# A graph network on one core: ScalarE instead of SP begins the loads of the source one-hots, three steps ahead instead of two

## The chip, the cores and the metric

The kernel runs on one core of one Trainium2 chip. The metric is the time of the whole program on the device in microseconds (us), as the median of several runs. Apart from that there is one profiled execution, from which all rows come. In the profile PE is TensorE, PEld its weight load, DVE VectorE, ACT ScalarE, POOL GpSimd and SP the engine that only issues transfers; a q behind a name (ACTq, SPq) marks work of that engine's sequencer, such as issuing a DMA.

## What is computed

The reference applies four graph networks one after the other to 12,500 nodes with 64 features each, over the same 212,500 edges (source, destination, type 0 to 3, weight), and normalizes the node rows after each:

```python
edge_index = jnp.stack([src, dst])
x = _layernorm(x + _L0_gnn_ref(x, ..., src, dst, edge_type_4), axis=-1)   # 4 steps: typed messages, GRU cell
x = _layernorm(x + _L1_gnn_ref(x, edge_index, ...), axis=-1)              # 2 GIN layers
x = _layernorm(x + _L2_gnn_ref(x, ...), axis=-1)                          # GCN, batch norm
x = _layernorm(x + _L3_gnn_ref(x, edge_weight, ...), axis=-1)             # weighted mean of neighbours
```

What they share is the costly part, a gather by source and a sum by destination:

```python
msgs = transformed[etypes, src]
a = jax.ops.segment_sum(msgs, dst, num_segments=num_nodes)
```

## The kernel before

A setup (the first 3,690 us) sorts the edges into slots and writes one-hot matrices of their sources to HBM (src_onehots). Then come nine passes over all edges, p = 0 to 8: four steps of the first network, three for the second (the last layer takes two), one for the third, one for the fourth. A pass needs the node rows of the pass before: all of them lie in SBUF as rows_now, three bf16 parts per value.

A pass has two interleaved loops. **Steps** (102 a pass, class Step) do the gather by matrix product: a step has 8 pairs, each of two matmuls (L963) of a one-hot matrix with a slice of rows_now into one of two PSUM banks ps_pair; ScalarE copies each bank to the buffer raw (copy_pair, L1164), and after the eighth pair issues one DMA that writes raw to HBM, `bounce` (move_out, L1170). There are two raw buffers, and step n + 2 may use that of step n when its write has landed (raw_written). A step's one-hots, 256 KB, lie in one of three buffers, step n in buffer n mod 3 (oh_landed tells that they are there). **Tiles** (98 a pass, class At) do the sum by destination: tile jj reads its messages back from bounce in another order (load_msgs, L657, three buffers), GpSimd gathers left-over rows (L808), VectorE makes one-hots of destinations, TensorE sums them in ps_agg (L977 to L1006), and a chain of small operations makes the new node row: VectorE sums, TensorE turns, ScalarE copies (L1184), TensorE's first product (L1040 to L1042), ScalarE's gate (L1190), VectorE's candidate and so on to a row, whose three parts ScalarE (L1233, L1241) and VectorE (L1708) make and SP stores (L672).

Steps run 8 ahead of tiles (AHEAD_G). At a pass's start steps 0 to 7 run alone; after that tile jj runs together with step jj + 8, pair by pair, on TensorE and on ScalarE alike. The last eight tiles have no step.

Each engine runs its own list in order. SP's for a pass: wait for the last stores and for the sums of the last tile, load rows_now in seven pieces (L700, one semaphore each; in pass 8 a store of rows_now, L704, instead, after the semaphore ch_lo, which GpSimd's L834 counts up), four loads of edge records (L648), two loads of one-hots, then for each of the first eight steps one more, the load for step n + 2 when step n - 1 is summed:

```python
for a in range(AHEAD_G):
    s = Step(GSTEPS * p + a)
    if s.n > 0:
        sp.wait_ge(pair_summed, s.pairs())
    load_oh(Step(s.n + 2))
    if a == G_TILES:
        load_msgs(at, 0)
```

After that, for each tile: wait for the tile two before, load records and messages, wait for pair_summed, load one-hots, wait for the row parts of the tile three before and store them. TensorE's pair 0 of a step waits for oh_landed, and the first steps of passes 1 to 7 also for their piece of rows_now (rows_loaded). ScalarE's list for a tile (one_tile, L1243) is: copies 0 and 1, L1241, L1184, copies 2 and 3, L1190, copies 4 and 5, the candidate, copies 6 and 7, the write L1170, L1233; passes 3, 6 and 8 have a square root (L1215) in place of L1233 there.

DMAs that SP issues go to one queue, those of ScalarE to another, those of GpSimd to a third; all are worked off by the same 16 DMA engines.

Of the kernel before, what the change touches and what calls it, by code (L numbers as in the profile page):

```python
# [9 lines left out]
P = 128  # L10
# [29 lines left out]
G_TILES = 6  # L40
# [34 lines left out]
def build(nc, x, src, dst, edge_type, edge_weight, g_W, g_b, g_w_ih, g_w_hh, g_b_ih, g_b_hh,  # L75
# [472 lines left out]
    def _(sp):  # L548
# [85 lines left out]
        sp.wait_ge(full_known, 1)  # L634
        sp.sem_inc(setup_done, 1)

        def load_oh(s):
            sp.dma_start(oh_words[s.buf()], src_onehots.ap()[ds(s.group() * P, P),
                                                             s.chunk() * CHUNK * P // 2:(s.chunk() + 1) * CHUNK * P // 2]
                         ).then_inc(oh_landed[s.buf()], 16)  # L640

        def load_weights(at, more):
            n = (at.jj + more) % 3
            sp.dma_start(grec[n][0:ROWS], slots.ap()[ds(at.d(more) * TILE_SLOTS, TILE_SLOTS), :]
# [30 lines left out]
        def one_tile(at):  # L675
            sp.wait_ge(tile_summed, at.tiles(CREDIT_T - 1))
            sp.sem_inc(sp_ran, 1)
            known = isinstance(at.i, int)
            if at.p == P_SAGE and not (known and at.jj + 1 >= NT):
                load_weights(at, 1)  # L680
            if not (known and at.jj + 4 >= NT):
                load_recs(at, 4)
            if not (known and at.jj + 1 >= NT):
                load_msgs(at, 1)
            if has_step(at):
                s = step_of(at)
                sp.wait_ge(pair_summed, s.pairs())
                sp.sem_inc(sp_ran, 1)
                if not (known and at.jj + AHEAD_G + 2 >= GSTEPS):
                    load_oh(Step(s.n + 2, s.i))  # L690
            if not (known and at.jj <= 2):
                store_rows(At(at.p, at.jj - 3, at.i))

        def one_pass(p):
# [12 lines left out]
                load_recs(at, a)  # L707
            if p == P_SAGE:
                load_weights(at, 0)
            for a in range(2):  # L710
                load_oh(Step(GSTEPS * p + a))
            for a in range(AHEAD_G):
                s = Step(GSTEPS * p + a)
                if s.n > 0:
                    sp.wait_ge(pair_summed, s.pairs())
                load_oh(Step(s.n + 2))
                if a == G_TILES:
                    load_msgs(at, 0)
            one_tile(At(p, 0))
            one_tile(At(p, 1))  # L720
            one_tile(At(p, 2))
# [415 lines left out]
    def _(act):  # L1137
# [29 lines left out]
        def move_out(s):  # L1167
# [2 lines left out]
            act.dma_start(bounce.ap()[ds(s.group() * ROWS, ROWS), s.chunk() * SB * RUN:(s.chunk() + 1) * SB * RUN],  # L1170
                          raw[s.raw()][0:ROWS].rearrange("p i b f -> p (i b f)")).then_inc(raw_written[s.raw()], 16)

        def copy_turned(at):
            p = at.p
            if p == P_GIN2A:
                return
            act.wait_ge(sum_turned, turns(at))
            if p < P_GIN1:
                to, frm = turned[:, :], ps_turn[:, 0:3 * P]
            elif p in (P_GIN2B, P_SAGE):  # L1180
                to, frm = turned[0:H, 0:2 * P], ps_turn[0:H, 0:2 * P]
            else:
                to, frm = turned[0:H, 0:P], ps_turn[0:H, 0:P]
            a_(to, frm, ACT.Copy).then_inc(turned_copied, 1)  # L1184
# [58 lines left out]
        def one_tile(at):  # L1243
# [27 lines left out]
            one_pair(7)  # L1271
            if s is not None:
                move_out(s)
            if prev is not None:
                (root if normed else high)(prev)

        act.wait_ge(ones_set, 1)
        for p in range(NPASS):
# [3 lines left out]
            if p == P_SAGE:  # L1282
# [7 lines left out]
                for n in range(NCH + 2):  # L1290
# [11 lines left out]
                    if n >= 2:  # L1302
                        at = slice((n - 2) * CH, (n - 1) * CH)
                        act.wait_ge(ch_rest, n - 1)
                        a_(rows_now[:, at, H:2 * H], sq_of[:, at, :], ACT.Copy).then_inc(ch_mid, 1)
            for a in range(AHEAD_G):
                for m in range(PAIRS):
                    copy_pair(Step(GSTEPS * p + a), m)
                move_out(Step(GSTEPS * p + a))
            one_tile(At(p, 0))  # L1310
            long_loop(act, p, 1, one_tile)
            end, normed = At(p, NT - 1), p in (3, P_GIN2B, P_SAGE)
# [684 lines left out]
```

## Time and profile before

| | |
|---|---|
| median of 3 runs | 12191.25 us (12191.2 to 12294.9) |
| profiled execution | 12181.28 us, span 12179.4 us |
| mean granted TensorE clock | 0.764 of full speed |
| busy | PE 60%, PEld 43%, DVE 51%, ACT 36%, POOL 54% |
| DMA | 2042.70 MB, mean 168 GB/s; SP's queue 1117.02 MB, ScalarE's 689.26 MB |
| loads of one-hots | 918, 256.0 KB each, by SP |

The span is the time from the first to the last instruction of the profiled execution. A share is an average over the setup, in which the DMA engines do little, and nine passes of 850 to 1,050 us.

### The profile page before, as it was taken

How to read it: one execution, taken by the hardware profiler on the slowest of the kernel's cores; microseconds unless marked ns; L12 is line 12 of the kernel's file. 1: busy time of each engine (PE TensorE's matmuls, PEld its weight loads, DVE VectorE, ACT ScalarE, POOL GpSimd, SP SyncE). 2: the span in 40 equal slices, each digit the busy share in tenths (PEclk: the TensorE clock that was granted, in tenths of full speed). 3: DMA queues.
4: the chain of work that ended last, by engine and by line, in shares of the span. 5: the costliest groups of instructions: out<-in, count | busy, mean ns of one | idle time of the engine just before them, and what ended most of it. 6: DMA issues, size and time to landing. Idle time of an engine off the chain costs nothing.

```text
span 12179.4 us, 174906 instructions
## 1 busy us (share of the span) xinstructions
PE 7330.7 (60%) x53873; PEld 5276.8 (43%) x53874; DVE 6165.4 (51%) x20158; ACT 4414.1 (36%) x11121; POOL 6612.2 (54%) x6335
## 2 busy tenths in 40 slices
PE   3333333333326877777777776666666776664999
PEld 0000000000005765666666664554445554543888
DVE  6555555554545665655656772222223332224998
ACT  0000000000004555545547774554444554443444
POOL 3555555555544655555555554555664444554666
PEclk6666666666658998988998997886766776776999
DMA  2110100000018988988988887888987777885888
GB/s 92 38 32 28 31 27 23 31 28 31 28 36 227 252 229 242 241 225 240 238 230 230 227 214 220 233 236 226 253 243 202 207 207 201 224 229 152 226 226 205
DMA packets 1207353, 2042.70 MB, mean 168 GB/s; under 512 B 431620, under 2 KB 895979, under 8 KB 1200318
## 3 DMA queue, kind: packets, MB, share of 16 engines
q1 hardware_dynamic: 878942, 1117.02, 35.7%
q10 hardware_dynamic: 126656, 689.26, 16.3%
q0 software_dynamic: 200864, 225.45, 9.7%
q8 instruction: 449, 7.36, 0.3%
q14 instruction: 442, 3.62, 0.1%
HBM read 1246.93 MB, written 784.10 MB: 167 GB/s over the span
## 4 chain that ended last, share of the span: by engine, by line
PE 39%; DVE 18%; another core or an unknown queue 15%; issue 14%; ACT 8%; DMA 2%; DVEq 2%; SPq 1%; POOL 1%; ACTq 0%; POOLq 0%
PE ps_pair L963 13%; DVE work L1460 6%; ACT work L1164 6%; PE ps_agg L980 5%; DVE work L1455 3%; PE ps_agg L977 3%; PE ps_agg L983 3%; PE ps_agg L997 2%; PE ps_gate L1040 1%; DVE work L1614 1%; PE ps_gate L1042 1%; PE ps_agg L1000 1%; PE ps_agg L1006 1%; DVE work L1537 1%
## 5 line engine op out<-in xcount | busy, mean ns | idle before, releaser
L808 POOL DMA_INDIRECT work<-node_rows,work x4410 | 4722.3, 1071 | 3649.5 <-issue 1175.0
L1164 ACT ACTIVATE work<-ps_pair 120x384 bf16<-120x384 f32 x7344 | 3375.0, 488 | 5559.2 <-PE ps_pair L963 4899.5
L963 PE MATMUL ps_pair<-rows_now,work 128*128 128x192 bf16 x14688 | 2734.2, 277 | 2093.8 <-issue 888.8
L792 POOL DMA_INDIRECT slots<-work x1862 | 1832.8, 984 | 1721.1 <-DVE work L1518 1168.3
L963 PEld LDWEIGHTS ps_pair<-rows_now,work 128*128 128x128 fp8e4 x14688 | 1257.3, 105 | 2902.0 <-issue 2786.2
L1460 DVE CUSTOM_DVE_ANT_0 work<-work,ps_agg 128x384 bf16<-128x384 bf16 x1862 | 1021.4, 551 | 1487.0 <-remote 1306.3
L889 PE MATMUL ps_agg<-work,not_above 128*128 128x384 bf16 x1764 | 750.7, 426 | 1669.8 <-issue 1260.2
L889 PEld LDWEIGHTS ps_agg<-work,not_above 128*128 128x128 bf16 x1764 | 176.8, 100 | 2545.2 <-issue 1595.8
L1595 DVE TENSOR_TENSOR work<-iota_bf,dl_all 120x2048 bf16<-120x2048 bf16 x882 | 1074.5, 1218 | 14.6 <-POOL rows_now L834 7.3
L891 PE MATMUL ps_agg<-work,above 128*128 128x384 bf16 x1862 | 799.9, 435 | 468.1 <-DVE work L1455 358.7
L980 PE MATMUL ps_agg<-work 120*128 120x192 bf16 x6272 | 1021.4, 300 | 28.5 <-DMA work<-bounce 24.8
L997 PE MATMUL ps_agg<-work 128*128 128x192 bf16 (+1 forms) x7840 | 925.6, 251 | 0.0
L977 PE MATMUL ps_agg<-work 120*128 120x192 bf16 (+1 forms) x6272 | 847.3, 261 | 13.3 <-DMA work<-bounce 11.3
L980 PEld LDWEIGHTS ps_agg<-work 120*128 120x128 bf16 x6272 | 718.8, 121 | 72.1 <-issue 30.4
L997 PEld LDWEIGHTS ps_agg<-work 128*128 128x128 bf16 x7840 | 691.8, 99 | 5.3 <-issue 1.0
L1614 DVE TENSOR_SCALAR work<-iota,work 128x512 bf16<-128x512 int16 x1960 | 596.6, 371 | 47.2 <-DMA work<-slots 46.8
L1455 DVE TENSOR_SCALAR work<-iota,work 128x384 bf16<-128x384 int16 x1862 | 606.4, 330 | 3.8
L977 PEld LDWEIGHTS ps_agg<-work 120*128 120x128 bf16 x6272 | 589.6, 104 | 27.7 <-issue 15.5
L1659 DVE TENSOR_REDUCE agg_sb<-ps_agg 128x64 f32<-128x192 f32 x392 | 134.9, 344 | 865.1 <-PE ps_agg L1002 701.7
L1000 PE MATMUL ps_agg<-work 128*128 128x192 bf16 x1960 | 540.7, 290 | 3.9 <-DMA work<-node_rows,work 3.8
L1646 DVE TENSOR_REDUCE agg_sb<-ps_agg 128x256 f32<-128x768 f32 x392 | 371.6, 948 | 252.3 <-PE ps_agg L997 212.2
L983 PE MATMUL ps_agg<-work,hs 120*128 120x192 bf16 x4704 | 466.7, 249 | 4.7 <-DMA work<-bounce 3.3
(300 smaller groups left out, 8965.2 us busy)
## 6 DMA issues: line engine op xcount, KB each, us to landing
bounce<-work ACTq DMA_DIRECT2D x918, 727.5 KB
work<-bounce SPq DMA_DIRECT2D x882, 727.5 KB
work<-src_onehots SPq DMA_DIRECT2D x918, 256.0 KB
work<-node_rows,work POOLq DMA_INDIRECT x4410
work<-lo_rows SPq DMA_DIRECT2D x17, 2880.0 KB
node_rows<-stage SPq DMA_DIRECT2D x686, 48.0 KB
rows_now<-node_rows SPq DMA_DIRECT2D x42, 768.0 KB, 8.5
slots<-work POOLq DMA_INDIRECT x1862
```

The source lines that it names most:

```text
L792: pool.indirect_dma_start(out=slots.ap(), out_offset=bass.IndirectOffsetOnAxis(ap=addr[par][:, t, n:n + 1], axis=0), in_=win[par][t][:, n, ...
L808: pool.indirect_dma_start(out=ring[:, at.slot3() * LB + b, 0:3 * H], out_offset=None, in_=table_of(at.p), in_offset=bass.IndirectOffsetOnA ...
L889: mm(acc, not_above[:, :], hot[t][(n - 1) % 3], start=False, stop=True, skip_group_check=True)
L963: last = mm(bank[:, a * 3 * H:(a + 1) * 3 * H], oh[s.buf()][:, 2 * m + a, :], rows_now[:, s.chunk() * CHUNK + 2 * m + a, :], start=a == 0, ...
L977: mm(acc[:, k * AGG:k * AGG + width], doh_one[at.half()][0:ROWS, b * P:(b + 1) * P], rhs, start=b in (0, 2 * SB), stop=False)
L980: mm(acc[:, 0:3 * H], doh_one[at.half()][0:ROWS, b * P:(b + 1) * P], rhs, start=b == 0, stop=False)
L983: mm(acc[:, 0:3 * H], doh_three[at.half()][0:ROWS, (a * GB + b) * P:(a * GB + b + 1) * P], rhs, start=a + b == 0, stop=False)
L997: last = mm(acc[:, k * AGG:k * AGG + width], ohs[:, (b * K + k) * P:(b * K + k + 1) * P], rhs, start=False, stop=end and k % 2 == 1)
L1164: a_(raw[s.raw()][0:ROWS, m // 2, 2 * (m % 2):2 * (m % 2) + 2, 0:3 * H], ps_pair[m % 2][0:ROWS, 0:6 * H].rearrange("p (b f) -> p b f", b=2 ...
L1455: v.tensor_scalar(hot[t][n % 3], iota512[:, 0:NCLS], key[:, t, n:n + 1], None, ALU.is_equal).then_inc(hot_made[t], 1)
L1460: v.tensor_tensor_reduce(out=junk[(2 * n + t) % 3], in0=hot[t][n % 3], in1=ps_agg[t][:, 0:NCLS], scale=1.0, scalar=0.0, op0=ALU.mult, op1= ...
L1595: last = v.tensor_tensor(to, numbers(ROWS, GB), spread(dl_all[0:ROWS, ds(at.d(more), 1), :].rearrange("p o n -> p (o n)"), ROWS, GB), ALU. ...
```

## The change

The loads of the one-hots leave SP's list and stand in ScalarE's. At a pass's start ScalarE issues the loads of steps 0, 1 and 2, and after the write of each step n the load of step n + 3, whose buffer is that of step n. ScalarE has then copied all eight pairs of step n, so no further wait is needed. In the first eight steps SP no longer waits for anything but the writes that load_msgs needs.

```diff
@@ SP @@
-        def load_oh(s):
-            sp.dma_start(oh_words[s.buf()], src_onehots.ap()[...]
-                         ).then_inc(oh_landed[s.buf()], 16)
...
             if not (known and at.jj + 1 >= NT):
                 load_msgs(at, 1)
-            if has_step(at):
-                s = step_of(at)
-                sp.wait_ge(pair_summed, s.pairs())
-                sp.sem_inc(sp_ran, 1)
-                if not (known and at.jj + AHEAD_G + 2 >= GSTEPS):
-                    load_oh(Step(s.n + 2, s.i))
...
-            for a in range(2):
-                load_oh(Step(GSTEPS * p + a))
-            for a in range(AHEAD_G):
-                s = Step(GSTEPS * p + a)
-                if s.n > 0:
-                    sp.wait_ge(pair_summed, s.pairs())
-                load_oh(Step(s.n + 2))
-                if a == G_TILES:
-                    load_msgs(at, 0)
+            load_msgs(at, 0)
@@ ScalarE @@
+        def load_oh(s):
+            act.dma_start(oh_words[s.buf()], src_onehots.ap()[...]
+                          ).then_inc(oh_landed[s.buf()], 16)
...
             if s is not None:
                 move_out(s)
+                if not (isinstance(at.i, int) and at.jj + AHEAD_G + 3 >= GSTEPS):
+                    load_oh(Step(s.n + 3, s.i))
...
+            for a in range(3):
+                load_oh(Step(GSTEPS * p + a))
             for a in range(AHEAD_G):
                 for m in range(PAIRS):
                     copy_pair(Step(GSTEPS * p + a), m)
                 move_out(Step(GSTEPS * p + a))
+                load_oh(Step(GSTEPS * p + a + 3))
```

SP's list at the start of pass 1, before (L638 is the load of one-hots):

```order
L700 DMA rows_now<-node_rows 128x3072 [waits stored2,tile_summed,stored1,stored0]
L700 DMA rows_now<-node_rows 128x3072 x5
L700 DMA rows_now<-node_rows 128x384
L648 DMA work<-slots 128x40 x4
L638 DMA work<-src_onehots 128x1024 x2
L638 DMA work<-src_onehots 128x1024 [waits pair_summed] x7
L657 DMA work<-bounce 120x4x776 [waits raw_written0,raw_written1]
L638 DMA work<-src_onehots 128x1024 [waits pair_summed]
```

and with the change (its lines 689, 643 and 652 are 700, 648 and 657 before):

```order
L689 DMA rows_now<-node_rows 128x3072 [waits stored2,tile_summed,stored1,stored0]
L689 DMA rows_now<-node_rows 128x3072 x5
L689 DMA rows_now<-node_rows 128x384
L643 DMA work<-slots 128x40 x4
L652 DMA work<-bounce 120x4x776 [waits raw_written0,raw_written1]
```

The nine loads of one-hots between records and messages are gone, and with them the waits for pair_summed. ScalarE's list at the start of pass 2 with the change (before, the rows of L1155 are not there; L1145 is the copy, L1151 the write):

```order
L1227 ACTIVATE stage<-left_over 128x64 [waits rest_made]
L1155 DMA work<-src_onehots 128x1024 x3
L1145 ACTIVATE work<-ps_pair 120x2x192 [waits pair_summed,raw_written0]
L1145 ACTIVATE work<-ps_pair 120x2x192 [waits pair_summed] x7
L1151 DMA bounce<-work 120x3104 [waits pair_copied]
L1155 DMA work<-src_onehots 128x1024
```

Three loads stand ahead of the pass's first copy, and one behind each write. ScalarE's list around the end of one tile in pass 1, before:

```order
L1164 ACTIVATE work<-ps_pair 120x2x192 [waits pair_summed] x2
L1170 DMA bounce<-work 120x3104 [waits pair_copied]
L1233 ACTIVATE stage<-row 128x64 [waits stored1,row_made]
L1164 ACTIVATE work<-ps_pair 120x2x192 [waits pair_summed,raw_written0]
L1164 ACTIVATE work<-ps_pair 120x2x192 [waits pair_summed]
L1241 ACTIVATE stage<-left_over 128x64 [waits rest_made]
L1184 ACTIVATE turned<-ps_turn 128x384 [waits sum_turned]
```

and with the change:

```order
L1145 ACTIVATE work<-ps_pair 120x2x192 [waits pair_summed] x2
L1151 DMA bounce<-work 120x3104 [waits pair_copied]
L1155 DMA work<-src_onehots 128x1024
L1219 ACTIVATE stage<-row 128x64 [waits stored1,row_made]
L1145 ACTIVATE work<-ps_pair 120x2x192 [waits pair_summed,raw_written0]
L1145 ACTIVATE work<-ps_pair 120x2x192 [waits pair_summed]
L1227 ACTIVATE stage<-left_over 128x64 [waits rest_made]
L1170 ACTIVATE turned<-ps_turn 128x384 [waits sum_turned]
```

The load stands between the write and the high part of the row, and everything behind it is in the order of before.

## Rows read from the trace of the kernel before

**Rows 1.** The page: busy time, DMA engines in 40 slices (tenths), chain by engine.
```profile
PE 7330.7 (60%) x53873; PEld 5276.8 (43%) x53874; DVE 6165.4 (51%) x20158; ACT 4414.1 (36%) x11121; POOL 6612.2 (54%) x6335
...
DMA  2110100000018988988988887888987777885888
...
PE 39%; DVE 18%; another core or an unknown queue 15%; issue 14%; ACT 8%; DMA 2%; DVEq 2%; SPq 1%; POOL 1%; ACTq 0%; POOLq 0%
```
**Rows 2.** Waits over the span: who <- for whom: us, times, longest us.
```profile
PE ps_pair L963 <- ACT work L1164: 820.2, 1108, 3.6
...
PE ps_pair L963 <- DMA work<-src_onehots: 354.6, 9, 124.4
...
SPq L688 <- PE ps_pair L963: 3857.0, 702, 12.0
```
**Rows 3.** Timeline, start of pass 1: start us, us, engine, line [idle before <-releaser].
```profile
4555.83 0.26 ACT L1241 ACTIVATE stage<-left_over 128x64 bf16<-128x64 f32 x1 [0.29 <-DVE left_over L1703]
...
4557.40 0.28 ACT L1281 ACTIVATE rsqrt_n<-n_tmp 128x98 f32<-128x98 f32 x1
...
4558.77 3.56 SPq L700 DMA_DIRECT2D rows_now<-node_rows  x7
...
4562.37 1.96 SPq L648 DMA_DIRECT2D work<-slots  x4
4564.37 19.79 SPq L638 DMA_DIRECT2D work<-src_onehots  x5
...
4574.05 0.80 PE L963 MATMUL ps_pair<-rows_now,work 128*128 128x192 bf16 x4 [20.81 <-DMA work<-src_onehots]
```
**Rows 4.** L700's 49 loads of rows_now.
```profile
DMA to landing us min/median/max: 4.1/8.6/11.9
```
**Rows 5.** Timeline, start of pass 6.
```profile
9121.87 4.04 SPq L700 DMA_DIRECT2D rows_now<-node_rows  x7
...
9138.75 0.80 PE L963 MATMUL ps_pair<-rows_now,work 128*128 128x192 bf16 x4 [16.98 <-DMA work<-src_onehots]
```
**Rows 6.** Timeline, start of pass 8.
```profile
11189.56 3.71 POOL L834 TENSOR_TENSOR rows_now<-work,rows_now 128x896 bf16<-128x896 f32 x2
...
11199.09 14.05 SPq L638 DMA_DIRECT2D work<-src_onehots  x4
...
11208.41 0.80 PE L963 MATMUL ps_pair<-rows_now,work 128*128 128x192 bf16 x4 [89.72 <-DMA work<-src_onehots]
```
**Rows 7.** Timeline, start of pass 0.
```profile
3686.31 1.75 SPq L648 DMA_DIRECT2D work<-slots  x4
...
3691.24 0.80 PE L963 MATMUL ps_pair<-rows_now,work 128*128 128x192 bf16 x4 [124.39 <-DMA work<-src_onehots]
```
**Rows 8.** Timeline of ScalarE, end of step 3 of pass 1.
```profile
4600.74 0.87 ACT L1164 ACTIVATE work<-ps_pair 120x384 bf16<-120x384 f32 x2 [0.28 <-PE ps_pair L963]
4601.72 0.32 ACTq L1170 DMA_DIRECT2D bounce<-work  x1
4602.14 0.87 ACT L1164 ACTIVATE work<-ps_pair 120x384 bf16<-120x384 f32 x2 [0.53 <-PE ps_pair L963]
```
**Rows 9.** Timeline of pass 1: step 2, and the start of tile 0.
```profile
4584.44 0.32 ACTq L1170 DMA_DIRECT2D bounce<-work  x1
...
4593.73 0.49 ACT L1164 ACTIVATE work<-ps_pair 120x384 bf16<-120x384 f32 x1 [2.31 <-remote]
...
4596.87 0.32 ACTq L1170 DMA_DIRECT2D bounce<-work  x1
...
4616.13 0.35 SPq L657 DMA_DIRECT2D work<-bounce  x1
...
4622.67 0.80 PE L977 MATMUL ps_agg<-work 120*128 120x192 bf16 x4 [1.11 <-DMA work<-bounce]
```
**Rows 10.** ScalarE's groups, 3900 to 4400 us (pass 0): busy us, mean ns | idle before.
```profile
L1184 ACT ACTIVATE turned<-ps_turn 128x384 f32<-128x384 f32 x60 | 29.4, 490 | 10.7 <-PE ps_turn L1021 6.0 <-issue 4.6
L1190 ACT ACTIVATE gate<-ps_gate 128x128 f32<-128x128 f32 x61 | 16.9, 277 | 68.7 <-PE ps_gate L1042 51.9 <-issue 14.4 <-remote 2.4
...
L1241 ACT ACTIVATE stage<-left_over 128x64 bf16<-128x64 f32 x60 | 15.4, 256 | 6.4 <-DVE left_over L1703 6.4
```
**Rows 11.** Pass 3, 6440 to 7260 us: busy by engine (ACT fourth); ScalarE's gate.
```profile
6440.00:7260.00 820.00, 603.44 (x5481) 534.95 (x5479) 576.09 (x1971) 649.49 (x1435) 478.13 (x449) 0.94 0.86 228
...
L1190 ACT ACTIVATE gate<-ps_gate 128x128 f32<-128x128 f32 x89 | 24.7, 277 | 36.1 <-remote 21.5 <-PE ps_gate L1042 13.3 <-issue 0.7
```

More of the change, by code:

```diff
@@ L635, in _ @@
         sp.sem_inc(setup_done, 1)
-        def load_oh(s):
-            sp.dma_start(oh_words[s.buf()], src_onehots.ap()[ds(s.group() * P, P),
-                                                             s.chunk() * CHUNK * P // 2:(s.chunk() + 1) * CHUNK * P // 2]
-                         ).then_inc(oh_landed[s.buf()], 16)
         def load_weights(at, more):
@@ L1171, in move_out @@
                           raw[s.raw()][0:ROWS].rearrange("p i b f -> p (i b f)")).then_inc(raw_written[s.raw()], 16)
+        def load_oh(s):
+            act.dma_start(oh_words[s.buf()], src_onehots.ap()[ds(s.group() * P, P),
+                                                              s.chunk() * CHUNK * P // 2:(s.chunk() + 1) * CHUNK * P // 2]
+                          ).then_inc(oh_landed[s.buf()], 16)
         def copy_turned(at):
```

## The prediction

> **What bounds the kernel now.** I read the page first. TensorE is busy 60% of the span, no engine is over that, and from the thirteenth slice on the 16 DMA engines are at seven to nine tenths [rows 1]. The chain of waits that ended last goes through TensorE for 39% and VectorE for 18% [rows 1]. So the nine passes are bound by the way the engines hand work to each other, with the DMA engines nearly full behind them.
>
> Next I asked the list of waits for the transfer that the change moves. TensorE waited for a source one-hot load 9 times, 354.6 us in all, the longest 124.4 us [rows 2]. There are 102 loads in a pass and 918 in all, so 909 landed before they were needed. Nine waits for nine passes: each should stand at a pass's start, and the timelines confirm it. Pass 0 has the one of 124.39 us [rows 7], pass 8 one of 89.72 us [rows 6]; the other seven share 354.6 - 124.4 - 89.7 = 140.5 us, 20.1 us each, and pass 1 shows 20.81 [rows 3]. What such a wait is worth is not its length, since most of it covers other work at the pass's end; it is the part in which the one-hots alone were missing.
>
> In the middle of a pass two other waits matter. TensorE waits for ScalarE's copies of its pair sums 1108 times, 820.2 us, and SP waits for pair sums 702 times, 3857.0 us, before it may issue a one-hot load [rows 2]. SP's long wait costs nothing by itself.
>
> **Part 1: the loads at a pass's start leave SP's queue (a gain).** In pass 1 SP issues the seven loads of rows_now from 4558.77 on, four record loads from 4562.37, and only then, at 4564.37, the first one-hots; TensorE's first pair starts at 4574.05, released by them [rows 3]. They are last in the queue behind 4.7 MB of rows. The first piece of rows_now is enough for step 0, and the quickest landing of a piece took 4.1 us [rows 4]. ScalarE's work for the pass before ends at 4556.1, and with rsqrt_n, which pass 1 alone has, at 4557.7 [rows 3]. So its three loads (768 KB, as much as one rows piece) start ahead of the rows, and the rows piece is what comes last: 4558.77 + 4.1 + 0.2 for the release = 4563.1. The first pair starts 11.0 us earlier. From the first rows load to the first pair it is 15.3 us in pass 1 and, the longest, 9138.75 - 9121.87 = 16.9 in pass 6 [rows 3, 5]; the other five lie between 15.3 and 15.9, and the seven sum to 109.8. Less 7 x 4.3 that is 79.7 us.
>
> In pass 8 no rows are loaded, but SP stores rows_now (4.7 MB) when GpSimd's L834 has ended at 11193.3, then loads records, and the one-hots last; the first pair starts at 11208.41 [rows 6]. TensorE itself needs only the end of L834, and ScalarE will have issued its loads before that: 15.0 us. In pass 0 only four record loads (1.75 us) stand ahead [rows 7]: 1.8 us. Sum of part 1: 79.7 + 15.0 + 1.8 = 96.5 us.
>
> **Part 2: one more DMA issue on ScalarE in each of the first eight steps (a loss).** Here ScalarE and TensorE alternate copy and pair. ScalarE has 0.28 us of idle time before each two copies; across the step's end, where it issues the write to the bounce buffer (0.32 us), it has 0.53 [rows 8]. Both banks are full then, so TensorE has nothing to give. A second issue of 0.32 us with some 0.06 us of spacing adds 0.38 us a step. Not all eight count: tile 0 starts when its messages land (4622.67, released by work<-bounce), and their load was issued at 4616.13, when step 5 had been written [rows 9]. Steps 6 and 7 lie beside that. So 6 x 0.38 x 9 = 20.5 us; with all eight it would be 27.4, with none 0.
>
> **Part 3: what the earlier start runs into (a small loss).** Step 0 will end about 9 us after the first rows load, while rows still land (issued over 3.56 us, with 8.6 us the median to landing [rows 3, 4]), and its 727.5 KB write shares the DMA engines with them. An estimate from these: the rows are in by 13 us, the write by 15. Step 2 wants the buffer back at 4.3 + 2 x 5.2 = 14.7. Between 0 and 2 us in each of seven passes; I take 1, together 7 us.
>
> There is also a slow stretch: the write of step 2 is issued 4596.87 - 4584.44 = 12.4 us after that of step 1, where the next one takes 4.85, and copies in it wait up to 2.31 us for a sum [rows 8, 9]. I know no cause. It lies beside GpSimd's first gathers, whose start doesn't move, so I expect it to meet a later step and to cost the same 7.6 us.
>
> **Part 4: the middle of a pass (a smaller loss).** The load of step n + 3 is issued when step n has been copied; before, the load of step n + 2 when step n - 1 had been summed. It is the same buffer at nearly the same moment: the change of "two" to "three" is one of naming, and the load gains no lead. What does change is that ScalarE spends 0.38 us more between the write and the next step's first copy, in 91 of a pass's 98 tiles. Behind that issue are queued L1233, two copies, L1241 and L1184, and for L1184 TensorE's first product waits. In 60 tiles of pass 0 ScalarE idles 68.7 us before L1190, 1.1 us a tile, and 10.7 and 6.4 us before L1184 and L1241, together 0.29 a tile [rows 10]. The delay is taken up by these: most of it before L1184, the rest before L1190. That cover hides it in eight of nine passes. If the cover were gone, it would be 0.38 x 91 x 9 = 311 us. Pass 3 has less of it: ScalarE is busy 649.49 of 820 us, with two table loads a tile, and idles 36.1 us before L1190 in 89 tiles, 0.41 each [rows 11]. There I let half through, 0.19 x 91 = 17 us, between 0 and 35. On SP's side 256 KB less stand ahead of each load of messages. TensorE waits for messages at the start of a pass alone, so this is worth nothing, or half a microsecond a pass.
>
> **Sum.** 96.5 - 20.5 - 7 - 17 = 52 us. The profiled execution has a span of 12179.4 us and took 12181.3, so 12129. The median of the three runs shown, 12191.25, is 10 us above it, and my forecast for the changed kernel's median is **12140 us**, 0.4% faster. A change of 1%, about what a measurement of this kernel can tell from none, is 122 us.
>
> One page rule bears on part 1. The trace shows one queue alone at work in a pass's start, 5.5 MB in the 15.3 us before the first pair [rows 3], or 2.1 us for 768 KB at most. The Trainium skill, page "DMA: Bandwidth & Descriptors", section "Queues, rings and completion order", says that a DMA engine takes turns between the queues that have work for it. Were ScalarE's loads issued together with the rows, both would share, and by that rule the first pair would come up to 2.1 us later: 52 - 7 x 2.1 = 37 us. With ScalarE ahead by 1 to 3 us the sum above stands.
>
> **Rivals.**
> *The saving doesn't come* (12230 us). The first pair stays 15 us behind the first rows load, because early one-hots, last stores and rows share the same DMA engines and all end together. Then only the losses of parts 2 and 4 are left, 38 us. For it: these engines are at 8 or 9 tenths of their time [rows 1]. Against it: the one-hots are a seventh of the bytes. The skill's same page, section "Issuing engines are not separate DMA queues", says that issuing from several engines saves only the issuer's time; by that rule this rival is the outcome. What is saved here is a place in the order, which the rule doesn't speak of.
> *ScalarE's issue is on the path* (12435 us; slower). At each tile's start it delays L1233, the copies and L1184, and through them product, gate, candidate and the next tile's sums. Price: 311 us instead of the 17 of part 4. It decides from 0.06 us a tile, where the 52 us are used up, and makes the kernel 1% slower from 0.21 more than I charge. For it: TensorE waits for ScalarE's copies 1108 times [rows 2]. Against it: the idle time before L1190 [rows 10], and that copies 6 and 7 of a step come before the new issue.
> *More is gained than the sum* (12070 us). The slow stretch may find TensorE waiting anyway and cost nothing, up to 7 x 7.6 = 53 us; or a tile in the middle gets 0.1 us quicker, 82 us, as SP no longer stands at the pair sums and issues stores and messages earlier. For it: the DMA engines are nearly full. Against it: nobody is seen to wait for those transfers.
> *The change doesn't do what it says.* True for the lead in the middle of a pass; that is in the forecast and has no price.
>
> **Chances.** Forecast 0.59, between 12090 and 12190 by its bounds; no saving 0.13; issue on the path, wholly or in part, 0.12; more gained 0.16. Faster by over 1% (below 12069) takes three quarters of the last, 0.12; slower by over 1% (above 12313) two thirds of the third, 0.08; within 1% the rest, 0.80. The range leaves out about a tenth on either side: 12055 to 12280.
>
> **What would show it.** Right: in passes 1 to 7 the first pair starts some 4.3 us after the first rows load and waits for that; no wait for one-hots is left; in pass 8 it starts with L834's end; the first steps take 5.2 us each instead of 4.85; tiles in the middle keep their time, and ScalarE's idle time before L1190 shrinks. Wrong: the first pair is still 15 us behind, or the tile's mean time moves by more than 0.1 us in most passes, which would outweigh all the rest.

## The result, and the profile after

The changed kernel takes 12366.84 us (median of 4 runs, 12343.31 to 12395.38) against 12218.01 us of the kernel before (4 runs beside it): ratio 1.0112, 95% interval 1.0058 to 1.0167. It is 1.1% slower, where the forecast was 12140 us and the range ended at 12280. The profiled execution took 12370.74 us with a span of 12368.9, which is 189.5 us more than before. In the experiments below, one execution of e9 (17731.88 us) and one of e11 (14694.56 us) ran far slower than all others of the same kernel and are in no ratio.

The page of the changed kernel: busy time, DMA engines in 40 slices, the chain by engine.

```profile
PE 7387.1 (60%) x53873; PEld 5351.8 (43%) x53874; DVE 6168.0 (50%) x20158; ACT 4365.2 (35%) x11121; POOL 6561.7 (53%) x6335
...
DMA  2110100001018878887888987887898887885898
...
PE 38%; DVE 16%; another core or an unknown queue 16%; issue 14%; ACT 10%; DMA 2%; ACTq 2%; DVEq 1%; POOL 0%; SPq 0%; POOLq 0%
```

The work is the same; what grew is ScalarE's part of the chain, from 8% to 10%, with 2% for its queue [rows 1]. The list of waits of the changed kernel (who <- for whom: us, times, longest):

```profile
PE ps_pair L944 <- ACT work L1145: 1153.0, 1207, 8.4
...
PE ps_pair L944 <- DMA work<-src_onehots: 124.2, 2, 122.9
...
PE ps_pair L944 <- DMA rows_now<-node_rows: 75.3, 7, 13.1
```

Waits for one-hots are left in pass 0 (122.9 us) and once for 1.3 us; in passes 1 to 7 TensorE now waits for the rows. Its waits for ScalarE's copies grew by 333 us [rows 2]: that is the first sign of the loss.

**The starts came out as forecast.** The timeline of the changed kernel at the starts of passes 0, 1, 6 and 8:

```profile
3684.10 1.75 SPq L643 DMA_DIRECT2D work<-slots  x4
...
3687.11 0.80 PE L944 MATMUL ps_pair<-rows_now,work 128*128 128x192 bf16 x4 [122.86 <-DMA work<-src_onehots]
...
4639.06 0.36 ACTq L1155 DMA_DIRECT2D work<-src_onehots  x1
...
4639.45 0.94 ACTq L1155 DMA_DIRECT2D work<-src_onehots  x2
...
4639.94 4.04 SPq L689 DMA_DIRECT2D rows_now<-node_rows  x7
...
4647.05 0.80 PE L944 MATMUL ps_pair<-rows_now,work 128*128 128x192 bf16 x4 [11.90 <-DMA rows_now<-node_rows]
...
9397.25 5.26 SPq L689 DMA_DIRECT2D rows_now<-node_rows  x7
...
9402.52 0.80 PE L944 MATMUL ps_pair<-rows_now,work 128*128 128x192 bf16 x4 [5.36 <-DMA rows_now<-node_rows]
...
11365.67 3.71 POOL L815 TENSOR_TENSOR rows_now<-work,rows_now 128x896 bf16<-128x896 f32 x2
...
11369.69 0.80 PE L944 MATMUL ps_pair<-rows_now,work 128*128 128x192 bf16 x4 [74.90 <-POOL rows_now L815]
```

From the first rows load to the first pair it is 7.1 us in pass 1, where ScalarE's three issues begin 0.9, 0.5 and 0.0 us before SP's first, 5.3 in pass 6 and 4.5 to 4.7 in the other five; the seven sum to 35.1, where it was 109.8 [rows 3, 5]. In pass 8 TensorE starts 0.3 us after GpSimd's last L815, where it was 15.1 [rows 6], and in pass 0 it is 3.0 us from the first record load to the first pair, where it was 4.9 [rows 7]. Pass 0 starts 4.1 us earlier in all; the other 2.2 us lie in the setup, which the change doesn't touch.

**The first eight steps.** ScalarE's timeline in pass 1: the end of a step, and the slow stretch.

```profile
4651.08 0.87 ACT L1145 ACTIVATE work<-ps_pair 120x384 bf16<-120x384 f32 x2 [0.28 <-PE ps_pair L944]
...
4652.05 0.35 ACTq L1151 DMA_DIRECT2D bounce<-work  x1
...
4652.43 0.41 ACTq L1155 DMA_DIRECT2D work<-src_onehots  x1
...
4652.94 0.87 ACT L1145 ACTIVATE work<-ps_pair 120x384 bf16<-120x384 f32 x2 [0.99 <-PE ps_pair L944]
...
4663.09 0.35 ACTq L1151 DMA_DIRECT2D bounce<-work  x1
...
4668.40 0.35 ACTq L1151 DMA_DIRECT2D bounce<-work  x1
...
4679.63 0.49 ACT L1145 ACTIVATE work<-ps_pair 120x384 bf16<-120x384 f32 x1 [2.31 <-remote]
4680.22 0.35 ACTq L1151 DMA_DIRECT2D bounce<-work  x1
```

Across a step's end ScalarE idles 0.99 us instead of 0.53, and a step takes 4668.40 - 4663.09 = 5.31 us instead of 4.85 [rows 8, 9]. The slow stretch is still there, now 11.8 us and two steps later, with the same idle time of 2.31 us [rows 9].

**The middle of the passes is where the time went.** The next view gives, for TensorE's pair matmuls alone, the stretch, its length, busy time (count) of PE and PEld, granted clock, DMA share, GB/s. Sixteen pair matmuls are one step, and there is one step a tile. The stretches lie in passes 0, 1, 2 and 6. Before:

```profile
3800.00:4400.00 600.00, 193.63 (x1160) 95.67 (x1160) 0.97 0.95 253
4850.00:5350.00 500.00, 161.49 (x928) 80.86 (x928) 0.94 0.92 241
5800.00:6300.00 500.00, 161.44 (x948) 79.89 (x947) 0.96 0.93 245
9650.00:10100.00 450.00, 145.13 (x712) 66.85 (x712) 0.72 0.78 206
```

Changed:

```profile
3800.00:4400.00 600.00, 183.49 (x1051) 92.67 (x1050) 0.93 0.88 227
4850.00:5350.00 500.00, 152.10 (x858) 77.04 (x856) 0.92 0.88 224
5800.00:6300.00 500.00, 155.09 (x856) 79.67 (x856) 0.89 0.87 222
9650.00:10100.00 450.00, 148.82 (x780) 67.35 (x780) 0.80 0.82 226
```

600 / (1160 / 16) = 8.28 us a tile before, 600 / (1051 / 16) = 9.13 after: 0.85 more in pass 0, 0.70 and 0.91 in passes 1 and 2, and 0.88 less in pass 6. The granted clock, a mean over its two levels of 2.4 and 1.2 GHz, is lower in the three passes that got slower and higher in pass 6. Over about 93 tiles these four passes give (0.85 + 0.70 + 0.91 - 0.88) x 93 = 147 us. Taken over the whole middle, from the first pair of step 8 to that of step 101, passes 0 to 2 lost 245 us, pass 6 gave 79 back, and the other five lost 53 together: 220 us.

ScalarE's groups from 3900 to 4400 us (pass 0) in the changed kernel:

```profile
L1170 ACT ACTIVATE turned<-ps_turn 128x384 f32<-128x384 f32 x55 | 27.0, 491 | 6.1 <-PE ps_turn L1002 4.2 <-issue 1.7
L1176 ACT ACTIVATE gate<-ps_gate 128x128 f32<-128x128 f32 x54 | 15.0, 278 | 89.0 <-PE ps_gate L1023 44.1 <-remote 37.0 <-issue 8.0
...
L1227 ACT ACTIVATE stage<-left_over 128x64 bf16<-128x64 f32 x55 | 14.1, 256 | 1.6 <-DVE left_over L1694 1.0
```

The forecast was that the idle time before the gate would shrink from 1.1 us a tile [rows 10] as it took up the delay. It grew to 89.0 / 54 = 1.65, by a kind that had hardly been there: "remote" (an idle time that ends by a release the profile can't place), 37.0 us in 14 gates. On average that is 2.6 us. The timeline shows one of them:

```profile
4087.26 0.49 PE L1023 MATMUL ps_gate<-typed_v,turned 128*128 128x192 f32 x2
...
4087.58 0.33 PE L944 MATMUL ps_pair<-rows_now,work 128*128 128x192 bf16 x2
...
4088.01 0.49 ACT L1145 ACTIVATE work<-ps_pair 120x384 bf16<-120x384 f32 x1 [1.42 <-PE ps_pair L944]
...
4088.65 0.32 PE L944 MATMUL ps_pair<-rows_now,work 128*128 128x192 bf16 x2 [0.41 <-ACT work L1145]
...
4090.88 0.28 ACT L1176 ACTIVATE gate<-ps_gate 128x128 f32<-128x128 f32 x1 [2.37 <-remote]
4091.05 0.87 ACT L1145 ACTIVATE work<-ps_pair 120x384 bf16<-120x384 f32 x2
```

and the stretches around it, with all engines (PE, PEld, DVE, ACT, POOL, then the clock):

```profile
4084.00:4088.00 4.00, 3.50 (x35) 3.18 (x32) 1.98 (x6) 1.92 (x6) 3.08 (x4) 1.00 0.84 192
4088.00:4092.00 4.00, 1.22 (x12) 0.80 (x11) 0.74 (x4) 1.62 (x5) 1.39 (x2) 0.85 0.95 340
4092.00:4096.00 4.00, 4.00 (x27) 3.71 (x26) 3.08 (x12) 1.99 (x6) 0.79 (x1) 0.50 0.48 98
```

Copy 4 stands behind the gate, pair 6 needs copy 4, and TensorE falls to 1.22 of 4 us busy; its clock is then granted at half (0.50, 1.2 GHz) for the next 4 us. So this late gate is paid twice. Behind eleven of the 14 the granted clock falls to half before the next gate, behind three it doesn't.

The rows also show on which side the delay lies. The gate waits for one count alone, gate_summed, and only TensorE's L1023 raises it. The trace has L1023 ending at 4087.75, 3.1 us before the gate starts; over the 14 late gates it is 1.7 to 3.2 us, over the other 40 the median is 0.04 us. The counts of pairs 4 and 5, whose matmuls stand at 4087.58 and 4088.65, arrive only at 4090.89 and 4090.97, right behind the gate's. So copy 4 couldn't have run earlier either, even with nothing ahead of it: what comes late is TensorE's report of its work (the ends of its matmuls are modelled in the profile), and ScalarE only shows it. The longer wait before the gate is 1.65 - 1.13 = 0.52 of the 0.85 us a tile; how the rest divides isn't shown.

### The profile page after: what moved, and what is told of

It is laid out like the page before. It is cut to its first block, busy times and chain, and to the rows that moved or that the text cites. A ratio compares the mean times of both kernels' runs of the same rounds, so it can differ in the third digit from the quotient of the medians.

```text
span 12368.9 us, 174060 instructions
## 1 busy us (share of the span) xinstructions
PE 7387.1 (60%) x53873; PEld 5351.8 (43%) x53874; DVE 6168.0 (50%) x20158; ACT 4365.2 (35%) x11121; POOL 6561.7 (53%) x6335
## 4 chain that ended last, share of the span: by engine, by line
PE 38%; DVE 16%; another core or an unknown queue 16%; issue 14%; ACT 10%; DMA 2%; ACTq 2%; DVEq 1%; POOL 0%; SPq 0%; POOLq 0%
PE ps_pair L944 13%; ACT work L1145 7%; DVE work L1451 6%; PE ps_agg L961 5%; DVE work L1446 3%; PE ps_agg L958 3%; PE ps_agg L964 3%; PE ps_agg L978 3%; ACTq L1155 1%; PE ps_gate L1021 1%; PE ps_gate L1023 1%; PE ps_agg L981 1%; DMA bounce<-work 1%; PE ps_agg L987 1%
## 5 line engine op out<-in xcount | busy, mean ns | idle before, releaser
L789 POOL DMA_INDIRECT work<-node_rows,work x4410 | 4668.0, 1058 | 3894.7 <-PE ps_agg L978 1171.2
L1145 ACT ACTIVATE work<-ps_pair 120x384 bf16<-120x384 f32 x7344 | 3367.0, 488 | 5371.0 <-PE ps_pair L944 4637.2
L978 PE MATMUL ps_agg<-work 128*128 128x192 bf16 (+1 forms) x7840 | 976.8, 260 | 0.0
L958 PE MATMUL ps_agg<-work 120*128 120x192 bf16 (+1 forms) x6272 | 881.1, 268 | 14.8 <-DMA work<-bounce 12.4
L978 PEld LDWEIGHTS ps_agg<-work 128*128 128x128 bf16 x7840 | 729.9, 103 | 10.8 <-issue 1.0
L1712 DVE SCALAR_TENSOR_TENSOR cand<-gate,ps_gate 128x64 f32<-128x64 f32 x392 | 86.8, 221 | 888.4 <-ACT gate L1176 501.5
```

The source lines that it names most:

```text
L789: pool.indirect_dma_start(out=ring[:, at.slot3() * LB + b, 0:3 * H], out_offset=None, in_=table_of(at.p), in_offset=bass.IndirectOffsetOnA ...
L958: mm(acc[:, k * AGG:k * AGG + width], doh_one[at.half()][0:ROWS, b * P:(b + 1) * P], rhs, start=b in (0, 2 * SB), stop=False)
L978: last = mm(acc[:, k * AGG:k * AGG + width], ohs[:, (b * K + k) * P:(b * K + k + 1) * P], rhs, start=False, stop=end and k % 2 == 1)
L1145: a_(raw[s.raw()][0:ROWS, m // 2, 2 * (m % 2):2 * (m % 2) + 2, 0:3 * H], ps_pair[m % 2][0:ROWS, 0:6 * H].rearrange("p (b f) -> p b f", b=2 ...
```

## The experiments

Each was run beside the kernel before; ratios are to that. Theory A: ScalarE's time at this place of a tile is on the path. Its rivals: a load on ScalarE's queue costs wherever it is issued; SP's order; the transfer itself. The table gives the ratio, us a tile in passes 0, 1, 2 and 6 worked out as above (same stretches, but 9250 to 9700 us for pass 6 of e5), and the "remote" idle time before pass 0's gate with its count, from 3900 to 4400 us.

| run | ratio (95%) | p 0 | p 1 | p 2 | p 6 | gate late |
|---|---|---|---|---|---|---|
| before | | 8.28 | 8.62 | 8.44 | 10.11 | 2.4, 1 |
| changed | 1.0112 (1.0058-1.0167) | 9.13 | 9.32 | 9.35 | 9.23 | 37.0, 14 |
| e7 changed again | 1.0114 (1.0076-1.0152) | 9.19 | 9.26 | 9.57 | 9.30 | 51.4, 18 |
| e1 starts only | 0.9964 (0.9946-0.9982) | 8.39 | 9.22 | 8.77 | 10.18 | 0 |
| e2 issue, all passes | 1.0105 (1.0076-1.0135) | 9.28 | 9.50 | 9.15 | 9.14 | 38.3, 15 |
| e3 changed, late issue | 1.0033 (1.001-1.0055) | 8.40 | 9.25 | 9.20 | 10.18 | 2.4, 1 |
| e4 changed, SP waits | 1.0088 (1.0057-1.0119) | 9.28 | 9.48 | 9.32 | 9.55 | 46.7, 16 |
| e5 starts and pass 6 | 0.9892 (0.9858-0.9927) | 8.25 | 8.32 | 8.47 | 9.47 | 0 |
| e6 starts and late | 1.0012 (0.9988-1.0036) | 8.28 | 9.35 | 8.93 | 10.11 | 2.4, 1 |
| e8 issue, 3 passes | 1.0167 (1.0129-1.0206) | 9.13 | 9.52 | 9.35 | 9.94 | 43.4, 17 |
| e9 two copies | 1.0046 (1.0026-1.0067) | 8.48 | 8.97 | 9.22 | 10.34 | 2.4, 1 |
| e10 one copy | 1.0021 (0.9996-1.0046) | 8.41 | 9.30 | 9.26 | 10.23 | 0 |
| e11 starts, copies in 6 | 0.9885 (0.983-0.9941) | 8.39 | 9.03 | 8.73 | 9.18 | 2.4, 1 |
| e12 e5 again | 0.9872 (0.9842-0.9902) | 8.38 | 8.83 | 8.95 | 9.49 | 0 |
| e13 three copies | 1.0206 (1.0166-1.0245) | 9.06 | 9.31 | 9.30 | 9.89 | 38.7, 16 |
| e14 issue behind copy 1 | 1.0053 (1.003-1.0076) | 8.41 | 9.17 | 8.79 | 9.89 | 2.4, 1 |
| e15 issue ahead of gate | 1.0046 (1.002-1.0071) | 8.28 | 9.17 | 9.11 | 10.03 | 0 |
| e16 transfer by SP | 1.0094 (1.0061-1.0126) | 8.65 | 9.22 | 9.30 | 10.06 | 0 |

The kernel before ran at 12434 us beside e1 to e4 and e9 to e12, and at 12210 to 12219 beside the others, so passes 1 and 2 are compared within these two groups only. The one profile of the kernel before belongs to the faster group; in the slower one pass 0 alone begins some 50 us later (3738 to 3747 us, against 3687 to 3697), and what passes 1 and 2 of the kernel before take there is not known.

Nor do these times follow the mean granted clock alone. TensorE's pair matmuls from 3800 to 4400 us in e9, then in e7:

```profile
3800.00:4400.00 600.00, 193.20 (x1132) 95.27 (x1130) 0.93 0.93 245
```

```profile
3800.00:4400.00 600.00, 180.78 (x1045) 92.13 (x1046) 0.95 0.86 226
```

e9 has the lower clock, 0.93, and 8.48 us a tile; e7 has 0.95 and 9.19.

**e1**, before with this piece of the change alone:

```diff
@@ ScalarE, pass start; SP's two loads are dropped, and its loop begins at a = 1 @@
+            for a in range(3):
+                s = Step(GSTEPS * p + a)
+                act.dma_start(oh_words[s.buf()], src_onehots.ap()[...]
+                              ).then_inc(oh_landed[s.buf()], 16)
```

> The kernel before, with one piece of the change: at each pass's start ScalarE begins the loads of the first three steps, and everything else stays with SP, two steps ahead. Theory A (ScalarE's own second issue costs the middle of the pass, and the starts are a gain): the pass starts gain as in the changed kernel, 3 to 13 us each and some 80 us in all, nothing is lost in the middle (passes 0 to 2 stay at 8.3 to 8.5 us a tile), so 12120 to 12150 us, ratio about 0.993. Theory B (what the middle loses comes from a shifted phase between passes and tiles, which anything at a start may cause): the middle of passes 0 to 2 goes to 9.2 us a tile here too, and the time is 12250 to 12400 us.

The starts alone gain 0.36%, 45 us, about half of A's 0.7%. Pass 0 is where A had it; passes 1 and 2 ran at 9.2 and 8.8 us. Whether the early starts did that is not shown, for the reason given above.

**e2**, before with an issue and nothing else:

```diff
                 move_out(s)
+                act.dma_start(spare.ap()[ds(s.n * P, P), :], eye_bf[:, 0:8]).then_inc(spare_written, 16)
```

> The kernel before, with a transfer that nobody reads (128 rows of 16 bytes to a spare array) begun on ScalarE where the change puts the step's load, in the tiles alone; SP still begins the loads. It takes ScalarE's issue time and nothing else from the change. Theory A (the issue is on ScalarE's path): 0.4 to 0.9 us a tile over 94 tiles in the passes that run at 8.3 to 8.5 us, so 12350 to 12600 us, passes 0 to 2 at 9.2 us a tile, and no gain at the starts. Theory B (the loss comes from the loads standing in ScalarE's queue, or from SP's order): within 0.3% of before.

One issue on ScalarE, of a transfer that nobody reads, brings back the changed kernel's whole picture: pass 0 at 9.28, the gate late 15 times, pass 6 faster. That is A, though 131 us where I had 160 and more, since pass 6 gives something back.

**e3**, the changed kernel with load_oh(s.n + 2) ahead of after_first, and not behind move_out.

> The changed kernel, with a tile's load issued on ScalarE after copies 2 and 3, ahead of the gate's first activation, where ScalarE waited 1.1 to 1.7 us in every tile of pass 0, and not behind the bounce store. The pass starts stay as changed, but for one load each. Theory A (issue time on the path): the issue falls in idle time, passes 0 to 2 go back towards 8.3 to 8.5 us a tile, and the time is 12100 to 12200 us. Theory B (any load on ScalarE's queue costs the same, wherever it is issued): passes 0 to 2 stay at 9.2 us and the time at 12370 us.

Pass 0 is back at 8.40 with one late gate, and pass 6 has lost its gain. The same load on the same queue costs nothing in pass 0 if it is issued in ScalarE's wait. But passes 1 and 2 stay at 9.2 and the whole is 41 us slower than before, where A had it no slower, so A doesn't explain these two passes.

**e4**, the changed kernel with SP's two lines for pair_summed put back, without a load.

> The changed kernel, with SP's wait for the summed pairs put back in each tile, without a load behind it, so that SP's stores and messages go out as late in the tile as before. Theory A (ScalarE's issue time): no change, 12350 to 12390 us. Theory C (SP, freed from this wait, begins stores and message loads earlier and these collide with GpSimd's gathers or the bounce): passes 0 to 2 go back to 8.3 to 8.5 us a tile, and the time is 12100 to 12200 us.

No change: SP's order is not the cause.

**e8**, e2's issue only where `at.p < 3`.

> The second experiment's kernel (before, with an unread small transfer issued on ScalarE behind each tile's bounce store), with that issue in passes 0 to 2 only. Theory A (the loss sits in passes 0 to 2, and pass 6 gives some 80 us back when the issue is there too): it costs at least as much as in all nine passes, 180 to 240 us, ratio 1.014 to 1.020, passes 0 to 2 at 9.2 to 9.5 us a tile, the others as before. Theory B (each tile of each pass pays about the same 0.15 us): a third of the second experiment's loss, ratio 1.0035.

It costs more in three passes than in nine: 204 us against 131. Pass 6 is at 9.94, against 9.14 in e2, which is 0.80 x 93 = 74 us, the size of the difference; since e2 and e8 ran in different groups, the match is not exact proof. A held.

**e7** and **e5**. In e5 SP skips the load in pass 6, and ScalarE has:

```diff
                 move_out(s)
+                if at.p == 6 and not (isinstance(at.i, int) and at.jj + AHEAD_G + 2 >= GSTEPS):
+                    load_oh(Step(s.n + 2, s.i))
```

> The changed kernel itself once more, on the chip of the others of this batch, as their yardstick. Theory A: ratio 1.006 to 1.017 as before, passes 0 to 2 at 9.2 to 9.4 us a tile with 30 to 50 dips of the granted clock each, pass 6 at 9.25 us. If the loss in passes 0 to 2 was a chance of that one profile, they are at 8.3 to 8.5 us here.

> The first experiment's kernel (the three loads of a pass's start on ScalarE, ratio 0.9964), and in the tiles of pass 6 alone ScalarE issues the load of two steps ahead behind the bounce store; the other passes' tiles leave it with SP. Pass 6 took 10.1 to 10.3 us a tile in before and in the two experiments without an issue behind the bounce store, and 9.2 to 9.35 in the changed kernel and in the two with one. Theory A (the place of the issue decides, in pass 6 as a gain): pass 6 at 9.2 to 9.4 us, some 80 us less than the first experiment, ratio about 0.990. Theory B (pass 6 depends on what an earlier pass left, or on three steps ahead): pass 6 stays at 10.2 us, ratio 0.9964.

Both nearly as A said: the ratios lie where A had them, pass 2 of e7 is at 9.57 and pass 6 of e5 at 9.47, each a little above A's range. TensorE's pair matmuls in e5, passes 0, 1 and 6 (columns as above):

```profile
3800.00:4400.00 600.00, 194.49 (x1164) 96.22 (x1164) 0.97 0.95 252
4850.00:5350.00 500.00, 163.32 (x962) 80.52 (x962) 0.96 0.94 249
9250.00:9700.00 450.00, 147.15 (x760) 66.82 (x760) 0.80 0.82 221
```

**e6**, e1 with e3's place for the tiles' loads.

> The first experiment's kernel, with all tiles' loads issued on ScalarE just ahead of the gate's activation, two steps ahead; the first eight steps leave them with SP. Theory A (an issue that falls into ScalarE's wait for the gate costs nothing): the time of the first experiment within 0.3%, ratio 0.995 to 0.999, so that the 0.7% between the first and the third experiment are the eight issues of each pass's start and the clock. Theory B (any load in ScalarE's tiles costs, wherever it stands): 1.000 to 1.004, as the third experiment.

Pass 0 is unharmed and passes 1 and 2 are slower. The ratio, 1.0012, lies in B's range and not in A's, though its interval reaches into both; A is right for pass 0 alone.

**e9, e10, e11**: is it time, or the issue? Copies into an unread tile stand where the issue stood, in passes 0 to 2 (e9 two, e10 one), or in pass 6 of e1 (e11):

```diff
                 move_out(s)
+                if at.p < 3:
+                    for n in range(2):
+                        a_(idle_out[:, n, :], eye_bf[:, 0:H], ACT.Copy)
```

> Before, with two small copies on ScalarE (128x64 each, into a tile that nobody reads) behind each tile's bounce store in passes 0 to 2, some 0.5 us in all by the 0.256 us of the 128x64 copies in the trace, and no transfer. All loads stay with SP. Theory A (it is ScalarE's time at this place, whatever fills it): as the issue in passes 0 to 2 did, ratio 1.012 to 1.019, those passes at 9.1 to 9.5 us a tile. Theory B (it is the issue of a transfer: its queue, its completion, its descriptors): within 0.4% of before.

> The same with one such copy, some 0.26 us a tile in passes 0 to 2. Theory A1 (every us of ScalarE's at this place is paid in the same proportion): half of what the two copies cost, ratio 1.006 to 1.010. Theory A2 (a point at which passes 0 to 2 tip from 8.4 to 9.3 us a tile, through the clock): either nearly nothing, below 1.004, or nearly all, above 1.012.

> The first experiment's kernel (starts on ScalarE, tiles with SP), with the two small copies behind the bounce store in pass 6 alone, and no load there. Theory A (pass 6 gains from a later ScalarE, by time alone): pass 6 at 9.2 to 9.5 us a tile, ratio about 0.990 as the fifth experiment. Theory B (it gains from the load leaving SP's queue): pass 6 at 10.2 us, ratio 0.996.

In pass 6 time alone gives the gain (9.18), as A said. In pass 0 two copies leave the gate in time and stand at 8.48; one copy stands at 8.41, e11 and e12 of the same group, which have nothing there, at 8.39 and 8.38. So two cost 0.1 us a tile and one nothing to speak of. A as I had stated it failed there: ratio 1.0046, not 1.012; and one copy is A2's "nearly nothing". **e12** is e5 once more.

> The fifth experiment's kernel once more (starts on ScalarE, in pass 6 the tiles' loads as well), beside the one with copies in pass 6. If the 1.1% that it won is its own and not that of one chip: ratio 0.986 to 0.993, pass 6 at 9.2 to 9.4 us a tile.

The ratio, 0.9872, is in the range; pass 6, at 9.49, again a little above it.

**e13 to e16**, all in passes 0 to 2: three copies; e2's issue behind copy 1; the same ahead of after_first; the same by SP behind its load of one-hots.

> Before, with three small copies (128x40, some 0.72 us in all) behind the bounce store in passes 0 to 2: more of ScalarE's time there than the issue of a transfer took (0.55 us), and no transfer. Theory T (ScalarE's time at this place decides, and 0.46 us of copies was just short of a point at which it tips): passes 0 to 2 at 9.2 us a tile or more, the gate's activation over 2 us late in 15 to 30 of a pass's 91 tiles, ratio above 1.014. Theory I (something in the issue itself): pass 0 at 8.6 to 8.9 us, the gate late in under 5 tiles, ratio 1.005 to 1.010.

> Before, with the small unread transfer in passes 0 to 2, issued on ScalarE behind copies 0 and 1 of a tile and no longer right behind the bounce store. Theory I1 (an issue costs most where it follows another on ScalarE's queue at once): pass 0 below 8.8 us a tile, ratio below 1.008. Theory I2 (any issue between the bounce store and the gate delays the gate's release, since its time or its transfer reaches it): pass 0 at 9.1 us or more, ratio 1.012 to 1.020.

> The same transfer in passes 0 to 2, issued just ahead of the gate's activation, where the trace of before shows ScalarE waiting 1.1 us. Theory (what falls into this wait is hidden in pass 0): pass 0 at 8.3 to 8.5 us, passes 1 and 2 at 8.6 to 9.1 as in the sixth experiment, ratio 1.001 to 1.008. If the transfer itself hurts wherever it is issued: pass 0 at 9.1 us, ratio above 1.012.

> The same transfer in passes 0 to 2, issued by SP behind its load of the one-hots: the transfer without ScalarE. Theory (neither 128 rows of 16 bytes nor one more issue on SP is felt): within 0.3% of before, passes 0 to 2 at 8.3 to 8.6 us. If the transfer is what hurts: ratio above 1.010.

ScalarE's added copies and its gate, 3900 to 4400 us, with two copies (e9), then with three (e13):

```profile
L1277 ACT ACTIVATE idle_out<-eye_bf 128x64 bf16<-128x64 bf16 x118 | 23.8, 248 | 28.6 <-ACT work L1165 18.7 <-issue 9.9
L1191 ACT ACTIVATE gate<-ps_gate 128x128 f32<-128x128 f32 x59 | 16.4, 278 | 76.2 <-issue 38.3 <-PE ps_gate L1043 35.4 <-remote 2.4
```

```profile
L1277 ACT ACTIVATE idle_out<-eye_bf 128x40 bf16<-128x40 bf16 x165 | 26.9, 225 | 26.5 <-ACT work L1165 21.8 <-issue 4.7
L1191 ACT ACTIVATE gate<-ps_gate 128x128 f32<-128x128 f32 x56 | 15.6, 278 | 84.9 <-PE ps_gate L1043 39.9 <-remote 38.7 <-issue 6.3
```

By the lists of groups two copies are 0.40 us a tile and three 0.49 (23.8 us for 118, 26.9 for 165, their overlaps taken off), less than I had expected. With a third copy and no transfer pass 0 tips from 8.48 to 9.06 us and 16 of 56 gates are late: it is time, with a tipping point between 0.40 and 0.49 us. (e9 and e13 ran in different groups; late gates in pass 0 appear in both, as e2 and e8 show.) Issued one or two places later the transfer of e2 doesn't do it (e14, e15; both inside what I1 and e15's theory gave for pass 0 and the ratio). In e16 ScalarE has nothing extra; pass 0 goes to 8.65, 0.37 us a tile more, with no late gate, and passes 1 and 2 to 9.2 and 9.3. The transfer as such is not what costs in pass 0, since e15 has the same one and stays at 8.28; that leaves its place in SP's list or queue, which no run separates. My expectation of e16, within 0.3%, was wrong.

## Why the prediction was wrong

**Part 1 (96.5 us) was right.** Passes 1 to 7 gained 109.8 - 35.1 = 74.7 (79.7 forecast), pass 8 14.8 (15.0), pass 0 1.9 (1.8): 91.4. Measured from the last step's first pair of the pass before, 20 us of this went into slower ends of passes. e1, with this part alone, is 0.36% faster. The rival "the saving doesn't come" is out.

**The rule of the Trainium skill**, page "DMA: Bandwidth & Descriptors", section "Issuing engines are not separate DMA queues", that issuing from several engines saves only the issuer's time, would have kept the starts at 15 us. They went to about 5 (35.1 / 7): the place in the order was worth it. By the section "Queues, rings and completion order", that an engine takes turns between queues, up to 2.1 us had to be allowed for; five of seven starts show 4.5 to 4.7, where 4.3 was worked out without it, and pass 1, with the loads nearly together, 7.1. Where the loads coincide the trace agrees that sharing costs, with 2.8 us over the 4.3 rather than 2.1.

**Part 2 (20.5 us) and part 3 (7 us) were right in kind, and small.** An issue costs 0.46 us a step, not 0.38. With the slow stretch moved, as forecast, the first eight steps of all passes lost 41 us, not 27.5: they took 459 us against 418. The two parts divide otherwise than forecast. e5 and e6, which start early but have no added issue in these steps, take 444 us for them, so some 26 us belong to part 3 and 15 to part 2.

**Part 4 (17 us) failed.** The step that failed reads: "The delay is taken up by these: most of it before L1184, the rest before L1190. That cover hides it in eight of nine passes." It took idle time that stands behind the delay as cover for whatever comes ahead of it. e15 and e3 show what the cover does hide in pass 0: an issue placed in it. An issue right behind the write, ahead of all of the next step's copies, is another matter: from 0.4 to 0.5 us on, TensorE's report for the gate is late in a quarter to a third of the tiles, the gate and copy 4 with it, TensorE idles before pair 6 and mostly comes back at half clock for some microseconds. Pass 3 had such gates before the change: 21.5 of the 36.1 us that the prediction counted as cover there were "remote" [rows 11]. In place of 17 us in pass 3 the middles lost 245 us in passes 0 to 2, and pass 3, where I had placed the loss, 20.

**The rival "ScalarE's issue is on the path" (0.12) was the outcome**, with a different build: not 0.38 us in each of nine passes, but some 0.85 in three, and pass 6 gives 0.88 back. e2 and e8 show both halves. The sum, with the 2.2 us of the setup: -91.4 - 2.2 + 20 + 41 + 220 = 187, and the span grew by 189.5. Pass 6 was not in any of my cases.

**Passes 1 and 2** are only half explained. In before they run at 8.4 to 8.6 us; each disturbance of them in the same group (e6, e14, e15, e16) brings them to 8.8 to 9.35, an SP transfer of 16-byte rows too. So in the changed kernel ScalarE's issue is sufficient there, not shown to be necessary. Only e5 kept them, at 8.3 and 8.5. Two more rows of the record say how far this reaches. Up to pass 5, e1, e5, e11 and e12 do the same work in the same order, and their pass 1 shows 9.22, 8.32, 9.03 and 8.83 us: one profile of these passes tells little. And in the stretches of passes 1 and 2 the changed kernel has 14 and 8 gates with a "remote" wait, while e6, e14, e15 and e16, nearly as slow there, have 0 to 2. So late gates are not needed for passes 1 and 2 to be slow; by what these are slowed is open.

**What stays open.** Why TensorE's report for the gate comes up to 3.2 us behind its matmuls once copies 0 to 3 are pushed back by 0.4 to 0.5 us: neither a load on ScalarE's queue, SP's order nor a transfer is needed for it (e4, e13), and what it meets was not found. Likewise why pass 6 runs better with a later ScalarE.

**A better version.** e5, with the starts on ScalarE and in pass 6 the tiles' loads too, has ratio 0.9892 and in the repeat 0.9872: 130 to 160 us under the kernel before, and 2.2% under the changed one.

## What to carry to other kernels

Move what stands last in a queue and is needed first: the first three loads of each pass were the gain, and the 99 behind them were the loss, but for pass 6. Don't count idle time that stands further down an engine's list as cover for work put ahead of it; in pass 0 the idle time before the gate hid an issue placed in it (e15), and not one placed behind the write. So try each place with an empty instruction before the real one. And read each pass by itself: one shift cost 0.85 us a tile in three passes and gave 0.88 back in a fourth, so the right place is chosen per pass.

## What was unexpected of the hardware

An issue of a DMA on ScalarE behind another took 0.41 us and made ScalarE's gap 0.46 us longer (0.99 against 0.53). A tile of pass 0 tipped from 8.48 to 9.06 us between 0.40 and 0.49 us of added ScalarE time, with 1 and 16 late gates. At the late gates of the changed kernel TensorE's report came 1.7 to 3.2 us behind the modelled end of its matmuls, where the median of the others is 0.04 us. After one stretch of 4 us with 1.22 us of TensorE work the granted clock was 0.50 for the next 4. An unread transfer of 128 rows of 16 bytes a tile, begun by SP, cost 0.94% where it ran in three of nine passes.
